# Layer norm in one VectorE pass a step later, gamma and beta on GpSimd, in a fused cross-attention kernel

## What is computed

```python
def _attention(query, key_value, W_qkv, b_qkv, W_o, b_o, ln_gamma, ln_beta):
    Q, K, V = ...            # projections with bias, split into 16 heads of 16
    scores = jnp.einsum('bhqd,bhkd->bhqk', Q, K) / np.sqrt(D_K)
    attn = jax.nn.softmax(scores, axis=-1)
    context = jnp.einsum('bhqk,bhkd->bhqd', attn, V)
    output = context @ W_o.T + b_o
    x = output + query
    mu = jnp.mean(x, axis=-1, keepdims=True)
    var = jnp.mean(jnp.square(x - mu), axis=-1, keepdims=True)
    return (x - mu) / jnp.sqrt(var + LN_EPS) * ln_gamma + ln_beta
```

## Time and profile before

| what | value |
|---|---|
| median of 3 runs | 214.79 us (213.75 to 216.98) |
| the profiled execution | 213.98 us |
| its span, first to last instruction | 212.0 us |
| mean granted TensorE clock | 0.986 of full speed |
| busy, share of the span | TensorE 89%, VectorE 83%, ScalarE 82%, GpSimd 72% |

### The profile page before, as it was taken

One profiled execution on the slowest core, in us unless ns is written; L12 is line 12 of the kernel. 1 busy time (PEld: TensorE's weight loads), 2 busy tenths in 40 slices (PEclk: granted clock), 3 DMA queues, 4 the chain that ended last, 5 costly groups with the idle time before them and its releaser, 6 DMA issues.

```text
span 212.0 us, 5573 instructions
## 1 busy us (share of the span) xinstructions
PE 187.8 (89%) x2052; PEld 170.8 (81%) x2052; DVE 175.1 (83%) x390; ACT 173.2 (82%) x313; POOL 152.5 (72%) x148
## 2 busy tenths in 40 slices
PE   0999899979999999989998999899989999898730
PEld 0998899869999988978897798879888988797530
DVE  6859985747787898989898989898989898883894
ACT  4578879979888989998999899989998999779330
POOL 9967540597447966896689668966896789879853
PEclk9999999999999999999999999999999999999995
DMA  6943531313566964795379446954694279211022
GB/s 202 341 99 114 149 57 45 119 63 101 176 157 159 235 214 87 201 240 171 90 184 242 152 85 177 243 156 94 167 230 111 60 200 250 58 52 53 4 97 99
DMA packets 32978, 30.39 MB, mean 143 GB/s; under 512 B 11306, under 2 KB 27672, under 8 KB 32952
## 3 DMA queue, kind: packets, MB, share of 16 engines
q1 hardware_dynamic: 31720, 28.78, 51.8%
q10 hardware_dynamic: 1232, 1.26, 2.0%
HBM read 11.32 MB, written 4.19 MB: 73 GB/s over the span
## 4 chain that ended last, share of the span: by engine, by line
PE 41%; POOL 22%; issue 15%; DVE 7%; ACT 6%; DMA 4%; SPq 2%; POOLq 0%; ACTq 0%; DVEq 0%
PE ps_x L414 16%; POOL p_l L1142 14%; PE ps_s L414 10%; PE ps_acc L414 9%; POOL result L1150 4%; PE ps_d L414 4%; ACT p_h L779 3%; DVE result L1008 3%; DMA q_mix<-q_high 3%; POOL rs_y L1163 2%; DVE xT_l L854 2%; DMA w_raw<-in_wkT 2%; SPq L316 1%; ACT ctx_h L786 1%; POOL rs_v L1157 1%
## 5 line engine op out<-in xcount | busy, mean ns | idle before, releaser
L1142 POOL TENSOR_TENSOR p_l<-p,p_h 128x512 f16<-128x512 f32 x80 | 95.1, 1194 | 42.8 <-ACT p_h L779 41.8
L959 DVE TENSOR_REDUCE maxima<-ps_d 128x4 f32<-128x308 f32 x128 | 57.1, 463 | 11.3 <-PE ps_d L414 9.5
L778 ACT ACTIVATE p<-ps_s 128x512 f32<-128x512 f32 x80 | 47.5, 593 | 10.3 <-PE ps_s L414 6.4
L779 ACT ACTIVATE p_h<-ps_s 128x512 f16<-128x512 f32 x80 | 47.3, 591 | 0.0
L414 PE MATMUL ps_s<-q_low,kblk 128*128 128x256 f32 x144 | 38.5, 288 | 1.8 <-issue 1.2
L414 PE MATMUL ps_acc<-vblk,p_h 128*128 128x34 f16 (+1 forms) x640 | 32.2, 182 | 0.8 <-POOL p_l L1142 0.7
L414 PEld LDWEIGHTS ps_acc<-vblk,p_h 128*128 128x128 f16 x640 | 27.8, 96 | 5.2 <-issue 2.0
L414 PE MATMUL ps_acc<-vblk,p_l 128*128 128x34 f16 (+1 forms) x320 | 30.2, 181 | 0.0
L414 PEld LDWEIGHTS ps_s<-q_low,kblk 128*128 128x128 f32 x144 | 27.1, 188 | 3.3 <-issue 1.6
L1008 DVE SCALAR_TENSOR_TENSOR result<-y,meanvar,rows_sb 128x256 f32<-128x256 f32 x30 | 28.5, 989 | 0.0
L414 PE MATMUL ps_s<-q_mix,kblk 128*128 128x256 f32 x96 | 26.4, 281 | 0.0
(11 more groups left out here) (107 smaller groups left out, 499.7 us busy)
## 6 DMA issues: line engine op xcount, KB each, us to landing
xT_raw<-in_xT SPq DMA_DIRECT2D x8, 512.0 KB, 3.5
x_rows<-in_x SPq DMA_DIRECT2D x16, 256.0 KB, 3.5
out_dram<-result SPq DMA_DIRECT2D x15, 256.0 KB, 2.1
q_mix<-q_lo SPq DMA_DIRECT2D x12, 256.0 KB, 4.8
kblk<-kT SPq DMA_DIRECT2D x64, 38.5 KB, 2.3
kblk<-kblk SPq DMA_DIRECT2D x6, 256.0 KB, 3.3
q_mix<-q_low SPq DMA_DIRECT2D x6, 256.0 KB, 4.7
q_mix<-q_high SPq DMA_DIRECT2D x6, 256.0 KB, 5.0
```

The lines of the kernel that those rows point to most:

```text
L778: nc.scalar.activation(p32[:, n % P32SLOTS], ps_s[n % 2][:], ACT.Exp, scale=SCALE)
L779: nc.scalar.activation(p_h[:, n % PSLOTS], ps_s[n % 2][:], ACT.Exp, scale=SCALE).then_inc(exp16, 1)
L959: v_.tensor_reduce(maxima[:, t, h0:h0 + DMAX_HEADS], ps_d[((DMAX + 1) * (s + 1) + j) % 2][:, 0:DMAX_HEADS * SKV] .rearrange("p (h k) -> p ...
L1142: g_.tensor_tensor(p_l[:, n % PSLOTS], p32[:, n % P32SLOTS], p_h[:, n % PSLOTS], ALU.subtract).then_inc(rest16, 1)
```

## The change

VectorE no longer centres at the end of a step. In the step after, behind maximum 3 and ahead of the statistics, `normalized` writes (y - mean) * root into `result` with two tensor_scalar instructions of 128x256; mean and root are both per-partition scalars, so there is one tensor input, `y`. GpSimd multiplies by gamma behind unit 2 (a new instruction of 128x512) and adds beta behind unit 3. ScalarE's scaling goes. That holds for the first 14 batches; batch 14 keeps the old way, with ScalarE, and batch 15 is finished by VectorE as before. `y` gets two slots and `result` three, and the store moves behind `load_mix` in the queue.

```diff
+RSLOTS = 3
+GAMMA_AT = 2
+DIRECT = B - 2
...
-                if S.store:
-                    if s < LAST_STEP:
-                        S.wait(sp, result_done, 1, -2)
-                        sp.dma_start(S.batch(out_v, 3, 0), result[:, (s - 3) % 2]).then_inc(st_out[(s - 3) % 2], 16)
...
                     load_mix(slot)
+                if S.store:
+                    if s < LAST_STEP:
+                        S.wait(sp, result_done, 1, -2)
+                        sp.dma_start(S.batch(out_v, 3, 0), result[:, (s - 3) % RSLOTS]).then_inc(st_out[(s - 3) % RSLOTS], 16)
...
-                    if u == (2 if S.project_q else 1) and S.store and s < LAST_STEP:
+                    if u == (2 if S.project_q else 1) and S.store and DIRECT <= s - 3 < B - 1:
...
+                def normalized():
+
+                    b = s - 3
+                    if b == 0:
+                        dve.wait_ge(ld_v[1], 16 * NSEG)
+                    S.wait(dve, root_done, 1, -2)
+                    if b >= RSLOTS:
+                        dve.wait_ge(st_out[b % RSLOTS], 16 * (b // RSLOTS))
+                    for t in range(QT):
+                        v_.tensor_scalar(result[:, b % RSLOTS, t], y_all[:, b % 2, t], meanvar_all[:, b % 2, t, 0:1],
+                                         rs_y[:, b % 2, t:t + 1], ALU.subtract, ALU.mult).then_inc(scaled, 1)
...
                 when(S.maxima, (max_of, 3))
+                when(S.store and s - 3 < DIRECT, (normalized,))
                 when(S.norm, (statistics, 0))
...
-                when(S.norm, (centre, 0), (centre, 1))
+                when(s == B, (centre, 0), (centre, 1))
...
-                    if u == (2 if s < B - 1 else 4) and S.store and s < LAST_STEP:
-
-                        r = result[:, (s - 3) % 2]
+                    r = result[:, (s - 3) % RSLOTS]
+                    if u == GAMMA_AT and S.store and s - 3 < DIRECT:
                         S.wait(pool, scaled, QT, -2 * QT)
+                        g_.tensor_tensor(r, r, gamma_sb.unsqueeze(1).broadcast_to([P, QT, D]), ALU.mult).then_inc(gamma_done, 1)
+                    if u == (GAMMA_AT + 1 if s - 3 < DIRECT else 4) and S.store and s < LAST_STEP:
+                        S.wait(pool, scaled, QT, -2 * QT)
+                        if s - 3 < DIRECT:
+                            S.wait(pool, gamma_done, 1, -2)
                         g_.tensor_tensor(r, r, beta_sb.unsqueeze(1).broadcast_to([P, QT, D]),
                                          ALU.add).then_inc(result_done, 1)
```

More of the change, by code:

```diff
@@ L226, in cross_attention_kernel @@
         ld_x = [sem(f"ld_x{n}") for n in range(2)]
-        st_out = [sem(f"st_out{n}") for n in range(2)]
+        st_out = [sem(f"st_out{n}") for n in range(RSLOTS)]
+        gamma_done = sem("gamma_done")
         st_last = sem("st_last")
@@ L403, in step @@
                     load_mix(slot)
+                if S.store:
+                    if s < LAST_STEP:
+                        S.wait(sp, result_done, 1, -2)
+                        sp.dma_start(S.batch(out_v, 3, 0), result[:, (s - 3) % RSLOTS]).then_inc(st_out[(s - 3) % RSLOTS], 16)
+                    else:
+                        for t in range(QT):
+                            sp.wait_ge(finished, t + 1)
+                            sp.dma_start(out_v[B - 1][:, t], result[:, (B - 1) % RSLOTS, t]).then_inc(st_last, 16)
             all_steps(step)
-            sp.wait_ge(st_out[0], 16 * B // 2)
-            sp.wait_ge(st_out[1], 16 * (B // 2 - 1))
+            for n in range(RSLOTS):
+                sp.wait_ge(st_out[n], 16 * len(range(n, B - 1, RSLOTS)))
             sp.wait_ge(st_last, 16 * QT)
@@ L944, in step @@
                 last = s == B + 1
-                own = int(last)
+                own = s % 2
                 stats, meanvar = stats_all[:, own], meanvar_all[:, own]
-                y_s = x_rows[:, (B - 1) % 2] if last else y[:]
+                y_s = x_rows[:, (B - 1) % 2] if last else y_all[:, own]
                 def accumulated(f):
@@ L986, in residual @@
                     if not last:
-                        S.wait(dve, centred, QT, -2 * QT)
+                        S.wait(dve, scaled, QT, -3 * QT)
                     v_.tensor_tensor(y_s.rearrange("p t d -> p (t d)"), ps_x[1][:],
@@ L1000, in centre @@
                 def centre(t):
[L1002 removed]
+                    o = (s - 2) % RSLOTS
                     if t == 0:
[L1004 to L1005 removed]
                         S.wait(dve, var_done, QT, -QT)
[L1007 removed]
+                        dve.wait_ge(st_out[o], 16 * ((s - 2) // RSLOTS))
                     v_.scalar_tensor_tensor(result[:, o, t], y_s[:, t], meanvar[:, t, 0:1], gamma_sb,
                                             ALU.subtract, ALU.mult).then_inc(centred, 1)
+                def normalized():
[5 more added lines that the diff above has]
+                        dve.wait_ge(st_out[b % RSLOTS], 16 * (b // RSLOTS))
+                    for t in range(QT):
+                        v_.tensor_scalar(result[:, b % RSLOTS, t], y_all[:, b % 2, t], meanvar_all[:, b % 2, t, 0:1],
+                                         rs_y[:, b % 2, t:t + 1], ALU.subtract, ALU.mult).then_inc(scaled, 1)
                 def context_lo_part(*halves):
```

20 lines of the change are left out of this document (8 added, 12 removed).

## The result

The changed kernel takes 237.53 us (median of 6 executions, 236.63 to 239.52) against 215.69 for the kernel before (6 executions beside it, 213.75 to 216.98): a ratio of 1.105, 95% interval 1.101 to 1.110. It is slower, as forecast, but 10 us above the 227.5 that were forecast, and outside the range of 217.5 to 232.0. The profiled execution took 236.63, its span is 234.7, and the mean granted clock 0.925 of full speed instead of 0.986.

What follows compares the result with a forecast made beforehand. TensorE was taken as the bound, busy 20.1 of 21.1 us a period. Odd steps 9.0, step 14 1.4, even steps 0 and tail 3.0 sum to 13.4 on 213.98: 227.4, stated as 227.5 us, range 217.5 to 232.

Steps and rivals of the forecast that it cites:

- The direction and the mechanism: Slower: GpSimd shuts out the pair ahead of maximum 4 and TensorE waits, net 1.5 us in each of six odd steps.
- near 0.8: Sign: the tensor_scalar group on VectorE would show a mean near 0.8 us and not 0.3.
- near 171: Sign: GpSimd would be busy near 171 us in the changed profile.
- some 2: Sign: the last unit of step 15 on GpSimd would come some 2 us later relative to its first.
- Removed parts worth nothing: L1008 in even steps and ScalarE's scaling worth 0; in odd steps L1008 worth at most 0.21 us, five times.
- 0.2 of waiting, 0.29 for instruction one: Odd steps: instruction one waits 0.2 us and runs 0.29; number two follows a 1.17 unit; 1.8 for the pair after overlap.
- shut out by two full units ... 2.6: Upper bound for one odd step: both instructions meet a full GpSimd unit of 1.17 us, net 2.6 us.
- Behind its end 0.4 is left, which is the pace of L1085: Prologue cast of 768 columns: 0.4 us remain after GpSimd's memset ends, read as L1085's pace; 0.29 taken per new instruction.
- The tail: From step 15: GpSimd's passes cost 2.0 us in step 15 and 1.0 in step 16, +3.0; bounds 1.3 and 3.9.
- Even steps at 0: Even steps 4 to 12: 0.3 us left of the pair against 0.21 gained at the query input; 0 together, 0.5 either way.
- Falls into gaps: GpSimd's second pass fits gaps ahead of unit 4, 1.19 us in odd and 0.88 in even steps; 0.3 sticks out.
- Free duration: A new tensor_scalar of 128x256 on VectorE, when not shut out, was taken at 0.29 us.

Runs made afterwards that it cites:

- e3: Changed kernel with VectorE's pair, in its place, replaced from batch 3 on by two bn_stats of 128x256 that GpSimd does not shut out: 221.93 us, ratio 1.033.
- e10: Changed kernel without its gamma pass, beta back behind unit 2, and the pair replaced by two bn_stats from batch 3 on: 220.13 us, ratio 1.021.
- e6: Kernel before with seven bn_stats (2.38 us of VectorE time) added ahead of maximum 4 in steps 3 to 16: 241.52 us, ratio 1.122.
- e12: Kernel before with VectorE's old pair L1008 cut to one column in steps 4 to 16: 212.74 us, ratio 0.991.
- e9: Changed kernel without its gamma pass on GpSimd, beta back behind unit 2, the pair left in place: 234.86 us, ratio 1.089.
- e5: Kernel of e2 with the store also moved behind the q_mix copies: 228.01 us, ratio 1.062.
- e2: Kernel before with one more GpSimd pass (gamma into a spare tile) behind unit 2 and beta behind unit 3: 233.47 us, ratio 1.085.
- e4: Kernel before with only the store moved behind the q_mix copies: 217.09 us, ratio 1.012.
- e8: Changed kernel with constants 0.0 and 1.0 in place of the pair's two per-partition scalars: one execution, 236.12 us.
- e11: Changed kernel without its gamma pass, the pair moved to the step's end and beta behind unit 4: 221.87 us, ratio 1.029.

## Why the prediction was off

- **The direction and the mechanism held.** The pair stands in the gapless run ahead of maximum 4, GpSimd shuts it out whole instructions long, and TensorE waits. L1022's mean is 874 ns ("near 0.8"), GpSimd is busy 168.8 us ("near 171"), the `q_mix` wait has gone, and the last unit of step 15 comes 2.8 us later relative to its first (218.69 - 210.62 beside the earlier trace rows; "some 2"). e3 and e10 confirm it: without the shut-out 15 us go; e6 shows that the delay alone is enough for the wait.
- **Removed parts worth nothing: held** (in the changed kernel the freed time shows as the 1.87 of waiting ahead of maximum 0; e12, with part of the pair's time gone and nothing in its place, gained 1%).
- **The step that failed first: "0.2 of waiting, 0.29 for instruction one".** I let the root end at 153.0, behind VectorE's arrival at 152.8, so that instruction one would run free and only number two meet a unit. In the trace the root is done, unit 0 starts at 114.30 and VectorE arrives at 114.41, 0.1 too late: instruction one meets a whole unit as well. 2.36 us instead of 1.8. This race was decided by 0.3 us, the prediction gave it one way, and its other end ("shut out by two full units ... 2.6") names what came, and as a bound it held: the net wait grew by 2.0 (2.70 - 0.44 - 0.27). The choice between the bounds was wrong. TensorE's idle time grew by 8.1 / 4 = 2.0 a period instead of 1.5, so this step is worth 1 to 2 us of the 9.3 by which the sum fell short in span.
- **The pace behind a shut-out was misread.** "Behind its end 0.4 is left, which is the pace of L1085": 0.41 us for 768 columns is 0.14 per 256, half of L1085's 0.294 for 256. The changed kernel shows the same: each of the pair ends some 0.15 behind its unit, not 0.29. This made the prediction's time too long, and so hid part of the race's miss.
- **The step that cost most: a term that was missing, the clock.** No part of the sum had it, although a wait five times as long as any in the steady state was forecast. TensorE's busy time grew by 3.3 us in four periods, 0.9 in step 14 and 3.4 in the tail, 7.6 of the 9.3 us (part of the tail's may lie beside waits). Behind each of the changed kernel's waits from step 5 on the clock fell; e6 shows that such a wait need not do that, so this term could have been forecast as a range, not as a number.
- **"The tail" at +3.0 was too high for what it counted and left out the rest.** It priced GpSimd's passes alone. They cost 1.4 us of waiting, by e3 and e10 (12.48 less 11.07 of TensorE's idle time) and by the changed kernel and e9 (13.47 less 12.00), near the lower bound of 1.3. The pair of step 15 it put at nothing: that waits 1.78 for the root, takes 2.34, and TensorE stands 2.76 for the normalized context (214.49). With the slow clock, granted 0.72 instead of 0.89, the tail came to 5.8, so that the 3.0 look nearer than they were.
- **Even steps at 0 held**: the pair costs 0.73 to 1.23 there and TensorE waits 0.42 for it at 82.50 and 0.27 at 154.29, and under 0.2 in the others.
- **"Falls into gaps" held for the changed kernel alone.** On the kernel before the same pass, with beta behind it, costs 13 to 19 us (e5, e2), of which 2.7 in e5 is the order of the queue (e4). I take the cover to come from two edits of the change, L1008's removal and the store's new place; the prediction did not say so, and no run takes the two apart.
- **Free duration**: 0.40 instead of 0.29, of which 0.12 is the scalar reads (e8). It moved nothing.

## What to carry to other kernels

A VectorE instruction that GpSimd shuts out costs what GpSimd is running at that moment, not its columns: place it where VectorE waits anyway (and price what its late result then holds up: 6 us here in e11), or give it a form that is not shut out, and if GpSimd has a run of instructions waiting, count one of them for each VectorE instruction. When a forecast wait of TensorE grows to several times those already there, leave room for the clock behind it, here 1.1 us each time that it fell; when a race between two engines is decided by less than the error of the times it is computed from, forecast both ends. And before an added pass is priced at nothing, say which other edit makes its gap.

## What the runs showed of the hardware that I had not expected

- One column is as bad as many: an instruction of 128x1 with two SBUF inputs took up to 1208 ns beside GpSimd and 208 ns at the shortest (e12, steps 5 to 15).
- A shut-out instruction ends some 0.15 us behind GpSimd's, though a free one takes 0.40 (1.205 us where the unit had 1.06 left to run): I read it as its start-up lying beside the wait.
- A wait of TensorE can cost more than itself, and its length alone doesn't say whether. Behind the waits of 1.1 to 1.3 us in the steady state the granted clock stayed at 1.00 (the period windows of e3 and e10). In the changed kernel it fell to 0.50 for three us and more behind every wait of 2.4 to 2.8. In e6 it fell behind four of the seven waits of 2.4 to 2.7 and not behind the other three. The wait of 1.94 at 71.03 of the changed kernel left it at 1.00, the one of 2.02 at 72.10 of e10 was followed by 0.50 from 74 to 76, and so was one of 1.49 in e5, from 78 to 81:

```profile
77.54 0.50 PE L416 MATMUL ps_x<-xT_h,wq_h 128*128 128x512 f32 x1 [1.49 <-DVE xT_l L856]
```

- The fall can come at once (at 118.00 in the changed kernel) or about 1 us behind the wait's end (at 202.11 there: 1.00 up to 203). Which waits it follows, and why, no run here settles.
